# A cross-network kernel's start: block 1's first layer moved behind block 0's second, its x in the shared tile, and zero matmuls in between

## What is computed

```python
h = x
for i, S in enumerate([128, 128, 128]):
    out = relu(einsum('bfd,bgd,fgs->bsd', x, h, W[i].reshape(39, Fk, S)) + b[i][None, :, None])
    if i != 2:
        h, direct = out[:, :64], out[:, 64:]
    else:
        direct = out
    outs.append(direct)
result = sum(concatenate(outs, axis=1), axis=-1)
```

## Time and profile before

| what | value |
|---|---|
| median of the runs | 563.03 us |
| the profiled execution's own time | 563.06 us |
| its span | 561.3 us |
| PE, DVE, POOL, ACT busy | 98%, 95%, 89%, 68% |
| chain that ended last | PE 82%, POOL 5%, DVE 3%, DMA 3% |
| granted clock | 1.00 |

### The profile page before, as it was taken

One profiled execution on the slowest core, in us unless ns is written; L12 is line 12 of the kernel. 1 busy time (PEld: TensorE's weight loads), 2 busy tenths in 40 slices (PEclk: granted clock), 3 DMA queues, 4 the chain that ended last, 5 costly groups with the idle time before them and its releaser, 6 DMA issues.

```text
span 561.3 us, 7869 instructions
## 1 busy us (share of the span) xinstructions
PE 550.6 (98%) x2020; PEld 378.3 (67%) x2020; DVE 533.3 (95%) x488; ACT 380.2 (68%) x436; POOL 498.0 (89%) x220
## 2 busy tenths in 40 slices
PE   7999999999999999999999999999999999999997
PEld 3444667777677776767776677777767676676765
DVE  5779999999999999999999999999999999999975
ACT  1263785777758586686777758587686777758563
POOL 1254999999999989999999999999999999999995
PEclk9999999999999999999999999999999999999999
DMA  8999936649195582936649195572927549162001
GB/s 320 411 411 364 395 112 236 250 151 355 59 324 200 170 318 92 364 105 240 248 154 359 48 325 195 188 297 99 348 113 273 228 143 365 53 222 99 2 1 37
DMA packets 29987, 121.74 MB, mean 217 GB/s; under 512 B 3600, under 2 KB 3728, under 8 KB 28048
## 3 DMA queue, kind: packets, MB, share of 16 engines
q1 hardware_dynamic: 29968, 121.52, 59.4%
HBM read 120.98 MB, written 0.52 MB: 216 GB/s over the span
## 4 chain that ended last, share of the span: by engine, by line
PE 82%; POOL 5%; issue 3%; DVE 3%; DMA 3%; SPq 2%; ACT 1%; POOLq 0%; DVEq 0%
PE acc L638 82%; POOL z_lo L302 5%; DMA xwide<-x 3%; DVE z_whole L453 1%; SPq L315 1%; DVE z_raw L453 1%; SPq L311 1%; ACT h L730 0%; DVE z_psum L453 0%; ACT w_hi L828 0%; ACT z_hi L727 0%; DVE sums L485 0%; ACT direct L730 0%; DVE sums L469 0%; POOL squares L579 0%
## 5 line engine op out<-in xcount | busy, mean ns | idle before, releaser
L302 POOL TENSOR_TENSOR z_lo<-z_raw,z_hi 128x1024 fp32r<-128x1024 f32 x198 | 468.7, 2406 | 30.8 <-ACT z_hi L727 29.9
L727 ACT CAST z_hi<-z_raw 128x1024 fp32r<-128x1024 f32 x198 | 204.6, 1048 | 98.1 <-DVE z_raw L453 92.9
L453 DVE TENSOR_TENSOR z_raw<-h,xwide 128x1024 f32<-128x1024 f32 x185 | 221.0, 1215 | 3.0 <-ACT h L730 2.9
L638 PE MATMUL acc<-z_hi,w_hi 128*128 128x512 f32 x550 | 198.0, 441 | 0.0
L638 PE MATMUL acc<-z_lo,w_hi 128*128 128x512 f32 x550 | 174.2, 398 | 3.2 <-POOL z_lo L302 3.0
L638 PE MATMUL acc<-z_hi,w_lo 128*128 128x512 f32 x518 | 165.4, 395 | 0.0
L638 PEld LDWEIGHTS acc<-z_hi,w_hi 128*128 128x128 f32 x550 | 103.5, 188 | 52.0 <-issue 32.5
L638 PEld LDWEIGHTS acc<-z_lo,w_hi 128*128 128x128 f32 x550 | 101.2, 188 | 33.2 <-POOL z_lo L302 10.1
L638 PE MATMUL acc<-z_whole,w_whole 128*128 128x512 f32 x256 | 120.0, 592 | 0.1
L638 PEld LDWEIGHTS acc<-z_hi,w_lo 128*128 128x128 f32 x518 | 97.1, 188 | 23.5
L302 DVE TENSOR_TENSOR z_lo<-z_psum,z_hi 128x1024 fp32r<-128x1024 f32 x77 | 93.7, 1217 | 3.6 <-ACT z_hi L727 2.5
(11 more groups left out here) (34 smaller groups left out, 173.6 us busy)
## 6 DMA issues: line engine op xcount, KB each, us to landing
xwide<-x SPq DMA_DIRECT2D x161, 512.0 KB, 5.1
xfirst<-x SPq DMA_DIRECT2D x13, 1792.0 KB, 8.5
xfirst<-x SPq DMA_DIRECT2D x15, 256.0 KB, 8.7
xfirst<-x SPq DMA_DIRECT2D x4, 512.0 KB, 11.9
xwide<-w SPq DMA_DIRECT2D x2, 1024.0 KB, 16.0
xfirst<-x SPq DMA_DIRECT2D x2, 768.0 KB, 11.1
xwide<-x SPq DMA_DIRECT2D x2, 768.0 KB, 9.7
w_whole<-w_whole SPq DMA_DIRECT2D x2, 256.0 KB, 13.8
```

The lines of the kernel that those rows point to most:

```text
L302: return eng.tensor_tensor(lo[:, 0:n, :], z[:, 0:n, :], hi[:, 0:n, :].bitcast(F32), ALU.subtract)
L453: nc.vector.tensor_tensor(dst, in0, in1, ALU.mult).then_inc(made[kind], 1)
L638: return nc.tensor.matmul(dst, weights, z[0:rows, t - G * g, :], start=first and first_g and t == G * g, stop=final and t == TILES[layer] - 1)
L727: nc.scalar.copy(z_hi[0:rows, slot("PV", pair, par, pos, HI_RING), 0:n, :], src).then_inc(hi_made, 1)
```

## The change

`ORDER_0` puts the ten groups of block 0's layer 1 first and block 1's layer 0 last; block 1's groups 1 and 3 become P and S, block 0's 12 becomes V and its 16 becomes P. `ORDER_1` is reordered, with kinds changed too. x of block 1 no longer has a tile of its own: it is loaded into `xfirst` once block 0's products are made, behind all of block 0's wide x. PE gets `BETWEEN` = 10 further zero matmuls between layer 0 of block 0 and step 0. `UNDER1_AT` goes from (0, 11) to (0, 8), `UNDER2_AT` from (1, 5) to (1, 6). In step 0 a V group's remainder comes one place behind it instead of two. ACT does block 1's `relu0` in step 1 at position 4, and `copy_xrep` and the squares are done for block 1 too.

```diff
-ORDER_0 = "00W 01W 02W 03W 11W 13W 10W 12W 16W 14W 15P 17W 18P 19V"
-ORDER_1 = ("00W 01W 22W 27W 20W 21W 02W 10P 11W 12V 23P 03S 13W 14P 24V 15P 16V 25P 17P 18P 19V "
-           "26P 28P 29V")
+ORDER_0 = "11W 13W 10W 12V 16P 14W 15P 17W 18P 19V 00W 01P 02W 03S"
+ORDER_1 = ("22W 27W 20W 21W 10P 11W 23P 12P 13W 24V 14P 25P 00V 01P 02W 15P 03S 16V 17P 18P 19V 26P "
+           "28P 29V")
+XREP_AT_0, SQUARE_AT_0, SQUARE_LOW_AT_0 = 9, 10, 12
+XREP_AT_1, SQUARE_AT_1, SQUARE_LOW_AT_1 = 9, 10, 14
+RELU0_AT_1 = 4
-UNDER1_AT, UNDER2_AT = (0, 11), (1, 5)
+UNDER1_AT, UNDER2_AT = (0, 8), (1, 6)
+BETWEEN = 10
...
# SP
-            load_first(1, xsecond_in[0], range(0, 1 + G), xsecond)
-            load_first(1, xsecond_in[1], range(1 + G, 1 + 2 * G), xsecond)
-            load_first(1, xsecond_in[2], range(1 + 2 * G, 1 + T0), xsecond)
...
             sp.wait_ge(*made_all(-1, 0))
-            load_first(2, xfirst_head_in[0], range(0, 1 + G))
+            load_first(1, xfirst_head_in[0], range(0, 1 + G))
+            load_first(1, xfirst_head_in[1], range(1 + G, 1 + 2 * G))
+            load_first(1, xfirst_in, range(1 + 2 * G, T0))
+            load_first(1, square_x_in, range(T0, 1 + T0))
             sp.dma_start(stage[2][:, 0:SPLIT_COUNT[2], :], w2).then_inc(w_staged[2], 16)
...
             for g in range(G12 - 4):
                 load_wide(1, 1, g)
+            sp.wait_ge(*made_all(0, 0))
+            load_first(2, xfirst_in, range(0, T0))
             sp.wait_ge(w1_lo_made, 2)
-            sp.wait_ge(whole_used, before("W", 1, 0))
+            sp.wait_ge(whole_used, before("W", 0, 8))
             for g in range(G12 - 2, G12):
                 load_wide(1, 1, g)
+            sp.wait_ge(square_lo_made, 1)
+            load_first(2, square_x_in, range(T0, 1 + T0))
             sp.wait_ge(w2_lo_made, 2)
-            sp.wait_ge(whole_used, before("W", 1, 6))
+            sp.wait_ge(whole_used, before("W", 1, 4))
...
# VectorE
-                        late.append((pos + V_LAG, pair, par, pos))
+                        late.append((pos + (1 if isinstance(j, int) and j == 0 else V_LAG), pair, par, pos))
...
# TensorE
+            for _ in range(BETWEEN):
+                nc.tensor.matmul(acc[2][:, :], zeros[:, 0:SIZE], zeros, start=True, stop=True)
             step(-1, 1)
...
# ScalarE
+                    if isinstance(j, int) and (j, pos) == (1, RELU0_AT_1):
+
+                        relu0(0, 1)
...
-                if isinstance(j, int) and j == 0:
-                    copy_xrep(1)
-                    relu0(j, par % 2)
```

More of the change, by code:

```diff
@@ L97, in before, with at @@
     return before(kinds, 3, 0) + (j - 3) * sum(e[2] in kinds for e in STEP) + here
+def at(j, name):
+    return {"xrep": {0: XREP_AT_0, 1: XREP_AT_1}, "square": {0: SQUARE_AT_0, 1: SQUARE_AT_1},
+            "square_low": {0: SQUARE_LOW_AT_0, 1: SQUARE_LOW_AT_1}}[name].get(
+                j if isinstance(j, int) else 3, {"xrep": XREP_AT, "square": SQUARE_AT, "square_low": SQUARE_LOW_AT}[name])
 def first_of(j, layer):
@@ L216, in cin @@
                  xwide[:, 1, T12 - 8:T12 - 4, :].rearrange("p a (b s) -> p (a b) s", s=SIZE)]
-        xsecond = xwide[:, 1, 0:1 + T0, :]
         w0_head = sums2[:].rearrange("p (t s) -> p t s", s=SIZE)
@@ L239, in cin @@
         xfirst_head_in = [sem("xfirst_head_in0"), sem("xfirst_head_in1")]
-        xsecond_in = [sem(f"xsecond_in{g}") for g in range(3)]
         xw_in = [[sem(f"xw_in{p}_{g}") for g in range(G12)] for p in range(2)]
@@ L406, in products @@
                     elif isinstance(j, int) and j == 0:
-                        if g < len(xsecond_in):
-                            dve.wait_ge(xsecond_in[g], 16)
-                    elif isinstance(j, int) and j == 1:
                         if g == 0:
@@ L414, in products @@
                             dve.wait_ge(xfirst_head_in[g], 32)
-                        elif g == len(xfirst_head_in):
+                        else:
                             dve.wait_ge(xfirst_in, 32)
                     elif g == 0:
[L418 to L423, removed]
+                        dve.wait_ge(xrep_ready, j + 1)
+                        dve.wait_ge(xfirst_in, 16 * (j + 2))
+                    if isinstance(j, int) and j < 0:
+                        in0 = xfirst[0:rows, 0:1, :].to_broadcast([rows, n, N])
                     else:
                         in0 = xrep_psum[0:rows, None, :].to_broadcast([rows, n, N])
-                        in1 = xshift[0:rows, G * g:G * g + n, :]
+                    in1 = xshift[0:rows, G * g:G * g + n, :]
                     if g == len(KINDS[0]) - 1:
@@ L563, in subtract @@
                 number = before("PV", j, pos)
-                if has_squares(j) and not any(e[2] == "P" for e in order(j)[SQUARE_LOW_AT:pos]) and pos >= SQUARE_LOW_AT:
+                if has_squares(j) and not any(e[2] == "P" for e in order(j)[at(j, "square_low"):pos]) and pos >= at(j, "square_low"):
                     pool.wait_ge(square_lo_made, before("S", j, place_of(j, 0)) + 1)
@@ L576, in square_low @@
                 n = before("S", j, place_of(j, 0))
-                pool.wait_ge(lo_made["P"], before("P", j, SQUARE_LOW_AT))
+                pool.wait_ge(lo_made["P"], before("P", j, at(j, "square_low")))
                 pool.wait_ge(square_made, 2 * n + 2)
@@ L586, in step @@
                         split_layer(2, len(SPLIT0) + 2).then_inc(w2_lo_made, 1)
-                    if pos == SQUARE_LOW_AT and has_squares(j):
+                    if pos == at(j, "square_low") and has_squares(j):
                         square_low(j)
@@ L623, in contract @@
                 first_g = g == first_of(j, layer)
-                bank = layer
-                if isinstance(j, int) and (layer, j) in ((0, 0), (2, BLOCKS)):
-                    bank = 2 - layer
+                bank = 0 if isinstance(j, int) and (layer, j) == (2, BLOCKS) else layer
                 dst = acc[bank][:, :]
@@ L644, in contract @@
                 if first_g:
[L645 to L649, removed]
+                    if isinstance(j, int) and (layer, j) == (2, BLOCKS):
                         pe.wait_ge(acc_read[0], BLOCKS)
@@ L666, in contract @@
                     return
-                if isinstance(j, int) and layer == 0 and j in (1, 2):
+                if isinstance(j, int) and layer == 0 and j in (0, 1):
                     pe.wait_ge(w_lo_made, len(SPLIT0) - 1)
@@ L742, in copy_xrep @@
             def copy_xrep(j):
-                if isinstance(j, int) and j == 1:
+                if isinstance(j, int) and j == 0:
                     act.wait_ge(xfirst_head_in[0], 32)
                 else:
-                    act.wait_ge(xfirst_in, 16 * (j + 1))
-                if not isinstance(j, int) or j > 1:
+                    act.wait_ge(xfirst_in, 16 * (j + 2))
+                if not isinstance(j, int) or j > 0:
                     act.wait_ge(*made_all(j - 1, 0))
@@ L770, in relu0 @@
                     act.wait_ge(*made_all(j, 1))
-                a = acc[2 if isinstance(j, int) and j == 0 else 0]
+                a = acc[0]
                 relu(h[0][0:HALF, :], a[0:HALF, :], 0, slice(0, HALF)).then_inc(h_ready[0], 1)
@@ L804, in step @@
                 for pos, (layer, g, kind) in enumerate(order(j)):
-                    if pos == XREP_AT and has(2, BLOCKS - 2):
+                    if pos == at(j, "xrep") and has(0, BLOCKS - 2):
                         copy_xrep(j)
-                    if pos == SQUARE_AT and has(1, BLOCKS - 2):
+                    if pos == at(j, "square") and has(0, BLOCKS - 2):
                         square(j)
-                    if pos == SQUARE_AT + 1 and has(1, BLOCKS - 2):
+                    if pos == at(j, "square") + 1 and has(0, BLOCKS - 2):
                         square_whole(j)
@@ L870 @@
     for p, f in enumerate(SQUARE_FIELD):
-        x0[0 if p < FIELDS else 2:, p, T0] = x[0 if p < FIELDS else 2:, f]
+        x0[0 if p < FIELDS else 1:, p, T0] = x[0 if p < FIELDS else 1:, f]
         w0a[p, T0 - 1] = w0[f, f]
```

4 lines of the change are left out of this document (removed).

## The result

The changed kernel takes 568.67 us (median of 6 runs, 567.94 to 570.93) against 563.01 of the kernel before (6 runs beside it): a ratio of 1.0105, 95% interval 1.0088 to 1.0123. It is slower, as forecast, but by 5.7 us where 1.3 were forecast, and outside the range of 562.4 to 566.2. The profiled execution took 568.57 us, its span is 566.7.

The account below looks back on a forecast made before the run. PE's work was taken as the bound. Paying 2.9 us between layers and 4.2 at weights, saving 2.5 of work and 4.0 of stalls, plus 0.7 from POOL's chain, gave +1.3: 564.3 us, range 562.4 to 566.2.

Parts of the forecast that it names:

- The bridge: The 10 zero matmuls between layers 0 and 1 take 2.33 us inside PE's 2.87 us wait; priced at nothing.
- 5.05 worked out: With x of block 1 out of the DMA queue ahead, all loads that followed land 5.05 us sooner.
- The wait at `12V`: PE's first split group of layer 1 waits for DVE's part of the low weights, 23.3 to 27.5, 4.2 us.
- `28P`: Group in step 1 where POOL's remainder was forecast just in time for PE, with no margin.
- three signs of being wrong: PE passes 12V before 26, a DMA ends a DVE wait between 17 and 27, or PE stands over 1 us in step 1.
- The new wait, on the path: PE stands before its first split group of layer 1 until both low-weight parts are there: 4.2 us.
- the 0.29 us operation at 27.5: DVE's part of the low weights, behind nine operations ending at 27.2, takes 0.29 us and ends at 27.5.
- rival 1: The clock falls in PE's stall at the low weights, costing 1.6 us on PE's path: 565.9; chance 0.26.
- The prediction's ledger: PE's account to step 2: 2.9 and 4.2 us paid, 2.5 of work and 4.0 of stalls saved, 0.6 later.
- Rival 3: Faster: the wait at 12V is short, low weights there before 25.1; at best 560.6 us; chance 0.12.

Follow-up runs that it names:

- e5: The e3 kernel with 17 zero matmuls on PE ahead of its wait for layer 1's low weights: 564.38 us (1.0027).
- e3: The changed kernel with DVE's subtraction for layer 1's low weights reading one input from PSUM, copied there by ACT: 566.19 us (1.0070).
- e4: The kernel before with DVE's part of layer 1's low weights one place later, position 12 instead of 11: 565.36 us (1.0040).
- e12: The changed kernel with DVE's part of layer 1's low weights at position 3 instead of 8, both inputs in SBUF: 568.01 us, timed once.
- e6: The e3 kernel with DVE's part of layer 1's low weights at position 3 instead of 8: 564.81 us (1.0026).
- e1: The changed kernel with DVE's part of layer 1's low weights one place earlier, position 7 instead of 8: 564.94 us (1.0042).
- e8: The e7 kernel without the 10 zero matmuls between the layers: 564.80 us (1.0023).
- e11: The e10 kernel without the 10 zero matmuls between layers 0 and 1: 562.28 us (0.9986).
- e10: The e7 kernel with DVE's layer 2 low weights part reading one PSUM input and ACT's block 0 layer 1 ReLU ahead of layer 2's rounding: 561.95 us (0.9982).
- e7: The changed kernel with groups 12 and 16 whole in step 0 and DVE's part of layer 1's low weights at position 7: 562.87 us (1.0004).

## Why the prediction missed

**What held.** PE's work is the bound of the loop and the start carries the difference: the start-up's last wait moved by 5.9 us, from 87.00 to 92.94, and the span grew by 5.4; where behind that wait the other 0.5 came back wasn't looked for. The bridge lies within the wait for the ReLU and costs nothing (14.69 to 17.56). The weights' rounding on ACT came at 17.42 instead of 22.24, right behind its ReLUs, so the weights had landed at least 4.8 us sooner (5.05 worked out). The wait at `12V` was named with its place, its releaser and its start. Step 1 ran without a listed PE wait until its group `28P`, where the forecast had no margin and PE stood 0.69 us (80.89). e5, which has only the steps that the forecast priced, came out at 564.38 against 564.3. None of the three signs of being wrong came: none of them watched the length of an operation.

**The step that failed** is the last term of "The new wait, on the path": "and the 0.29 us operation at 27.5". I took a duration from a row at 29.90 us without looking at what POOL did there. It was idle from 28.47 (24.22 + 4.25) to 31.02. In the new place POOL has a remainder to make at the very same time, and the operation took 2.48 us. Taking the hold away (e3) gave 2.5 us of the median. The Trainium skill (SBUF — State Buffer, Who interferes with whom) states that a DVE instruction with two SBUF inputs contends with a GpSimd instruction that reads SBUF, and that the port pair that they share is an exclusive lock; that the later one is blocked for the whole of the other's instruction it says of DVE's two-port modes. The traces agree, and show the whole-instruction hold for this operation too: 2.48, 2.34 and 3.54 us with both inputs in SBUF and POOL ahead (changed kernel, e4, e12), 0.29 with one in PSUM (e3, e6) or POOL idle (e1). It was the rule to look for, and I hadn't counted it among the rivals.

**The clock** was the second term: the forecast's sum put it at nothing and left it to rival 1, with a chance of 0.26 and a price of 1.6 us. The granted clock fell in each traced run in which PE stood 2.7 us or longer after the first work: e1, e3, e8, e11, e12 and the changed kernel. Against e5, where two split groups take 2.90 us (27.51 to 30.41) with the restart, it cost 5.28 - 2.90 = 2.4 us in the changed kernel, and in e1 and e3 1.5 and 1.3 on these groups (in e3 0.3 more on the whole group behind them), near the price. The windows show why: the clock was low for 6.8 us in the changed kernel, 5.3 of them under PE's work, and for 3.4 us in each of the other five. e3 against e5, which differ by the zeros alone, give 1.8 us of the median. So the chance was far too low. It doesn't need the hold: in e3, with a wait of 4.0 us, all four runs have a mean clock of 0.994 to 0.997, where those of e5 have 0.999 or 1.000.

**Sum.** In the trace of the changed kernel the wait ends 2.1 us later than in e5's (29.60 against 27.51) and the two groups behind it take 2.4 longer: 4.5. Step 1 starts 4.5 later (47.32 against 42.86), the last wait comes 4.4 later (92.94 against 88.50) and the span is 4.4 longer. With the 1.3 that was forecast this makes 5.8, against 5.7 measured.

**Counts.** The prediction's ledger counts 20 whole and 16 split groups before; `ORDER_0` and `ORDER_1` have 19 and 17, and three groups of five matmuls in either kernel, not two. The work removed is then 2.2 us and not 2.5, the stalls are 4.5 and not 4.0, and the ledger puts the start of step 2 0.4 later and not 0.6. POOL got two more remainders in step 1 (11 against 9), not three. The forecast of 564.3 doesn't rest on these counts.

**Rival 3** said that a sooner wait could make it faster, at 560.6, and that it takes an order in which the low weights are there by 25.1. e6 did that and ended at 562.5 in its lower group. In its trace the rounding of layer 2's weights runs from 35.05 to 36.95 and the ReLU comes behind it, at 36.97; I hadn't looked for that, since it was hidden by the stall. e10, which turns the two round in e7 and takes the second tie's cost away, gained 0.9 on e7.

**The spread** of the changed kernel's runs (567.94 to 570.93) fits a lost second tie in the slowest run. So do the runs some 2 us above the rest in e1, e3, e5 and e6, which have that tie too and in whose traces DVE won it. None of the upper runs has a trace, so this is argued, not shown.

## What to carry to other kernels

A duration from a trace belongs to the company it was measured in: before a small DVE operation with two SBUF inputs is moved, look at what POOL does at the new place, and give it a PSUM input or a gap in POOL's work if it is on the path. Here ACT's rounding and DVE's next product take about as long as each other, so POOL and DVE became ready within 0.01 us; where the loser of such a tie is held for a whole operation, the times fall into two groups. A stall of PE near 3 us is priced with a slow stretch behind it, and a stall hides what is late next, so its removal gives back less than its length.

## What was not expected of the hardware

- DVE's 64 x 128 subtraction with both inputs in SBUF: 0.29 us alone, 2.34 to 3.54 when it becomes ready 0.01 to 0.84 us behind the start of a POOL operation that reads SBUF. At 0.01 us it goes either way: held in the changed kernel, e8 and e12, not held at the second tie of e3 and e7. Where DVE wins, POOL's remainder takes 2.52 to 2.56 us instead of 2.34 to 2.41.
- The granted clock fell around waits of PE of 2.74 us (e8, e11), 2.82 (e12), 2.87 (e1), 4.0 (e3) and 6.2 (changed kernel). Only in e8 and the changed kernel did it fall while PE stood (2.3 and 4.6 us into the wait). In e1, e11, e12 and e3 it fell when PE was at work again, by 0.1, 0.4, 0.8 and 1.3 us; in e3 PE ran at full speed for that time and was then slowed (0.73 in the window 28 to 30, 0.50 from 30 to 32). Not every run loses clock at 2.7 us: 2 of the 10 of e8 and 4 of the 11 of e11 kept a mean of 1.000.
